# Flamingo block on one core: the softmax sums of the two query halves on separate PSUM rows, with every engine's order rewritten

## The reference, cut to what matters

```python
x = x + tanh(g_xattn[0]) * attention(layernorm(x), ctx, Wq, Wkv_expand, Wout)   # 16 batches x 256 x 512
x = x + tanh(g_ffn[0])   * ffn(layernorm(x), w_gate, w_up, w_down, ...)         # fp8-rounded, width 1408
# attention: 16 heads of 32, 256 queries, 256 keys, causal
scores = einsum('bhqd,bhkd->bhqk', qh, kh) / sqrt(32)
scores = where(tril, scores, lowest)
attn = softmax(scores, axis=-1)        # exp, then divided by its sum over the keys
out = einsum('bhqk,bhkd->bhqd', attn, vh)
```

## Time and profile before

| | |
|---|---|
| median of three runs | 728.0 us |
| the profiled execution | 729.19 us |
| its span, first to last instruction | 727.4 us |
| mean granted TensorE clock | 0.978 of full speed |
| busy share: PE, DVE, ACT, POOL | 90%, 93%, 76%, 74% |

### The profile page before, as it was taken

The page is one execution under the profiler, slowest core; times in us unless marked ns, Lnnn a source line. Parts: engine busy times, 40 slices in busy tenths (PEclk is TensorE's granted clock), DMA queues, the critical chain, the costliest instruction groups (busy, mean ns, idle before and its releaser), DMA issues.

```text
span 727.4 us, 15637 instructions
## 1 busy us (share of the span) xinstructions
PE 657.9 (90%) x6091; PEld 419.9 (58%) x6160; DVE 680.1 (93%) x1127; ACT 555.5 (76%) x995; POOL 538.5 (74%) x601
## 2 busy tenths in 40 slices
PE   1758698999999999999999999999999999998794
PEld 1647476666566666566565657566566556545342
DVE  4999998989899999999999999999999999999997
ACT  6896878987869787878878787979797867555642
POOL 6768889796968778687878686968696677666651
PEclk9888999999999999999999999999999999999997
DMA  8887768385795757585867566675775686512121
GB/s 303 223 153 199 157 147 176 80 176 94 123 158 107 152 105 154 80 181 96 167 108 141 111 144 116 132 144 114 155 123 116 90 150 100 111 22 87 27 70 58
DMA packets 143479, 93.57 MB, mean 129 GB/s; under 512 B 107598, under 2 KB 114126, under 8 KB 143406
## 3 DMA queue, kind: packets, MB, share of 16 engines
q1 hardware_dynamic: 141246, 90.74, 61.6%
q0 software_dynamic: 576, 1.45, 0.8%
q10 hardware_dynamic: 1584, 0.39, 0.3%
HBM read 31.59 MB, written 9.83 MB: 57 GB/s over the span
## 4 chain that ended last, share of the span: by engine, by line
PE 47%; DVE 29%; POOL 11%; DMA 5%; issue 3%; ACT 3%; SPq 0%; ACTq 0%; DVEq 0%
PE pair L1153 26%; DVE mx L3116 5%; POOL PT L793 4%; PE pair L1411 4%; PE pair L1416 3%; DVE room L2943 2%; DVE room L2947 2%; PE pair L1394 2%; DVE room L3260 2%; PE pair L1440 2%; DVE room L3308 2%; PE pair L1436 2%; POOL room L832 2%; DVE tm L3323 2%; DVE wmax L2962 2%
## 5 line engine op out<-in xcount | busy, mean ns | idle before, releaser
L832 POOL TENSOR_TENSOR room<-room,up_scale 128x512 f32<-128x512 f32 (+1 forms) x96 | 125.6, 1312 | 63.1 <-ACT room L2349 62.2
L3116 DVE TENSOR_REDUCE mx<-pair 128x6 f32<-128x768 f32 x128 | 117.6, 947 | 1.7 <-PE pair L1343 1.4
L793 POOL TENSOR_SCALAR_AFFINE_SELECT PT<-PT 128x512 f32<-128x512 f32 x128 | 104.0, 841 | 13.1 <-ACT PT L2274 13.0
L2274 ACT ACTIVATE PT<-pair 128x768 f32<-128x768 f32 x128 | 98.3, 814 | 9.4 <-PE pair L1394 7.8
L1153 PE MATMUL pair<-WgT,room 128*128 128x512 bf16 (+1 forms) x382 | 89.5, 366 | 2.5 <-DVE room L3447 0.8
L1153 PE MATMUL pair<-xT,WqTh 128*128 128x256 bf16 x512 | 86.5, 272 | 1.5 <-ACT WdT L2037 1.3
L1153 PE MATMUL pair<-WuT,room 128*128 128x512 bf16 (+1 forms) x368 | 84.8, 361 | 3.3 <-DVE room L3260 1.4
L2349 ACT ACTIVATE room<-room,sx 128x512 f32<-128x512 f32 (+1 forms) x96 | 65.2, 682 | 24.2 <-DVE room L3260 18.8
L1153 PE MATMUL pair<-WdT,room 128*128 128x512 bf16 x326 | 75.4, 379 | 3.1 <-DMA room<-room 2.9
L2381 ACT ACTIVATE room<-room 128x512 bf16<-128x512 f32 (+1 forms) x96 | 55.8, 586 | 21.2 <-DVE room L3308 21.1
L1153 PE MATMUL pair<-xT,WqTl 128*128 128x256 bf16 x256 | 69.7, 272 | 0.0
(11 more groups left out here) (151 smaller groups left out, 1863.4 us busy)
## 6 DMA issues: line engine op xcount, KB each, us to landing
xin<-in_x_dram SPq DMA_DIRECT2D x16, 512.0 KB, 4.0
x<-in_x_dram SPq DMA_DIRECT2D x16, 512.0 KB, 4.8
K<-kh SPq DMA_DIRECT2D x32, 256.0 KB, 4.9
Q<-qh SPq DMA_DIRECT2D x32, 256.0 KB, 4.6
out_dram<-x SPq DMA_DIRECT2D x15, 512.0 KB, 3.0
K<-kl SPq DMA_DIRECT2D x16, 256.0 KB, 6.1
Q<-kl SPq DMA_DIRECT2D x16, 256.0 KB, 4.2
room<-in_L_ffn_w_down_dram SPq DMA_DIRECT2D x4, 704.0 KB, 9.0
```

What stands on the lines that cost most here:

```text
L793: pool.affine_select(out=view, in_=view, compare_op=ALU.is_ge, fill=0.0, base=0, pattern=[[0, 2], [0, 2], [1, P]], channel_multiplier=-1). ...
L832: pool.tensor_tensor(g, g, up_scale[:, chunk(n)[1]], ALU.mult).then_inc(slw_done, 1)
L2274: act.activation(head_columns(ring(b, c), 0, 384), head_columns(shifted_pair[c][:, :], 0, 384), ACT.Exp, scale=SCALE).then_inc(exp_done, 1)
L3116: dve.tensor_reduce(mx[:, heads, :], head_columns(w, 0, 3 * P).rearrange("p h (r s) -> p h r s", s=P), AX.X, ALU.max).then_inc(max_done, 1)
```

## The change

The sums of queries 0 to 127 and of queries 128 to 255 no longer lie side by side in 256 columns, but on different rows of the same 128 columns. `pick` has eight variants instead of four, with a 1 in every eighth column. Variant g serves queries 0 to 127, variant 4+g serves queries 128 to 255. The diagonal pattern comes from a flat tile that is read with rows of 33. The number of streamed columns per head group is the same (1536 over the four column tiles), now in twelve matmuls of 128 columns instead of four of 256 and four of 128. The reciprocal has 128 columns instead of 256, and eight shuffles of 128 columns take the place of four of 256.

```diff
-        pick = sb("pick", [P, KT, HD])
+        pick_flat = sb("pick_flat", [P, TT * KT * (HD + 1)])
...
-        rsum = sb("rsum", [P, S])
+        rsum = sb("rsum", [P, P])
...
+        pick = pick_flat[:, 0:TT * KT * HD].rearrange("p (v c) -> p v c", c=HD)
+        pick_ones = pick_flat[:, :].rearrange("p (v c) -> p v c", c=HD + 1)
...
-            constant(pool.memset(pick[:, :, :], 0.0))
-            for g in range(KT):
-                constant(pool.memset(pick[:, g, :].rearrange("p (a b) -> p a b", b=4)[:, :, g:g + 1], 1.0))
+            constant(pool.memset(pick_flat[:, :], 0.0))
+            for a in range(HD // (TT * KT)):
+                constant(pool.memset(pick_ones[:, :, TT * KT * a:TT * KT * a + 1], 1.0))
...
-                for t in range(TT):
-                    for j in range(G):
-                        last = pe.matmul(sum_bank[HD * j:HD * j + HD, t * P:S], pick[:, g, :],
-                                         probabilities(b, 2 * g + j // 2, j % 2, t), start=(g == 0 and t == 0),
-                                         stop=(g == KT - 1 and t == TT - 1), skip_group_check=True)
+                for j in range(G):
+                    pe.matmul(sum_bank[HD * j:HD * j + HD, 0:P], pick[:, g, :], probabilities(b, 2 * g + j // 2, j % 2, 0)[:, 0:P],
+                              start=(g == 0), stop=False, skip_group_check=True)
+                for j in range(G):
+                    pe.matmul(sum_bank[HD * j:HD * j + HD, 0:P], pick[:, KT + g, :], probabilities(b, 2 * g + j // 2, j % 2, 0)[:, P:S],
+                              start=False, stop=False, skip_group_check=True)
+                for j in range(G):
+                    last = pe.matmul(sum_bank[HD * j:HD * j + HD, 0:P], pick[:, KT + g, :], probabilities(b, 2 * g + j // 2, j % 2, 1),
+                                     start=False, stop=(g == KT - 1), skip_group_check=True)
...
-                dve.reciprocal(rsum[:, :], sum_bank[:, 0:S]).then_inc(rsum_done, 1)
+                dve.reciprocal(rsum[:, :], sum_bank[:, 0:P]).then_inc(rsum_done, 1)
...
-                dve.stream_shuffle(out=R[:, 2 * h, :], in_=rsum[:, :], mask=[2 * h] * HD)
-                dve.stream_shuffle(out=R[:, 2 * h + 1, :], in_=rsum[:, :], mask=[2 * h + 1] * HD).then_inc(r_spread, 1)
+                for g in range(2 * h, 2 * h + 2):
+                    for t in range(TT):
+                        last = dve.stream_shuffle(out=R[:, g, tok(t)], in_=rsum[:, :], mask=[KT * t + g] * HD)
+                last.then_inc(r_spread, 1)
```

```diff
             x_low(3, 1)
             unit_rounded(13)
-            down_placed(7)
             down_placed(1)
-            unit_rounded(15)
-            down_placed(6)
+            down_placed(3)
+            rstd2_made(0)
             normalised_low(1, 0)
...
```

Some PSUM banks of the weight preparation and of the last batch's turning are others (`turned_bank`, `turned_x_bank`, `aw_bank`, `s_bank`, `w_bank`), and a few waits come or go with the order. One of them is on PE:

```diff
-                if n == 4 and b <= 10:
+                if n == 4 and 2 <= b <= 11:
                     pe.wait_ge(t_done, 6 * b + 1)
```

More of the change, by code:

```diff
@@ L834, in added @@
             def added(b, t):
+                if t == 0 and b == 0:
+                    pool.wait_ge(y_done, 1)
+                if t == 0 and b == 9:
+                    pool.wait_ge(y_done, 19)
                 if t == 0 and b >= 12:
@@ L986, in _ @@
             added(0, 1)
+            up_scaled(1, 5)
             causal_part(3, 2)
@@ L1105, in _ @@
             causal_part(14, 7)
+            rstd2_made(13)
             up_scaled(12, 5)
+            normalised_low(14, 0)
             added(12, 0)
-            normalised_low(14, 0)
             normalised_low(14, 1)
-            rstd2_made(13)
             up_scaled(13, 0)
@@ L1711, in _ @@
             values(3, 1)
+            gate_products(1, 0)
             down(0, 0)
+            scores(3, 0)
+            scores(3, 1)
             up_products(1, 0)
-            scores(3, 0)
-            gate_products(1, 0)
-            scores(3, 1)
+            projected(2, 0)
             scores(3, 2)
-            projected(2, 0)
             projected(2, 1)
@@ L1721, in _ @@
             scores(3, 3)
+            scores(3, 4)
             keys(4, 1)
-            scores(3, 4)
             gate_products(1, 1)
@@ L1861, in _ @@
             scores(13, 3)
+            keys(14, 0)
+            scores(13, 4)
+            keys(14, 1)
             projected(12, 1)
-            scores(13, 4)
-            keys(14, 0)
-            keys(14, 1)
             scores(13, 5)
+            scores(13, 6)
+            queries(14, 0)
+            scores(13, 7)
             gate_products(11, 1)
-            scores(13, 6)
             gate_products(11, 2)
-            scores(13, 7)
-            queries(14, 0)
+            up_products(11, 1)
+            gate_products(11, 3)
             queries(14, 1)
-            up_products(11, 1)
+            gate_products(11, 4)
+            turned_maxima(13)
+            up_products(11, 2)
             queries(14, 2)
-            up_products(11, 2)
-            turned_maxima(13)
-            gate_products(11, 3)
-            gate_products(11, 4)
             queries(14, 3)
@@ L1948, in _ @@
             down(12, 0)
-            up_products(13, 0)
             scores(15, 1)
+            gate_products(13, 0)
             scores(15, 2)
-            gate_products(13, 0)
+            scores(15, 3)
             projected(14, 0)
-            scores(15, 3)
             scores(15, 4)
@@ L1958, in _ @@
             scores(15, 6)
+            up_products(13, 0)
+            scores(15, 7)
             gate_products(13, 1)
-            scores(15, 7)
             up_products(13, 1)
+            gate_products(13, 2)
             values(15, 1)
-            gate_products(13, 2)
+            turned_maxima(15)
             gate_products(13, 3)
-            turned_maxima(15)
+            up_products(13, 2)
+            projected(14, 2)
             gate_products(13, 4)
-            projected(14, 2)
-            up_products(13, 2)
             gate_products(13, 5)
@@ L2478, in _ @@
-            unit_taken(5)
-            unit_abs(8)
-            unit_abs(10)
+            unit_abs(7)
+            unit_taken(5)
+            means1(2, 0)
+            keys_high(1, 0)
+            c_high(2)
+            keys_high(1, 1)
+            unit_abs(9)
+            squares1(2, 0)
+            means1(2, 1)
+            keys_exact(1, 0)
+            unit_taken(6)
+            keys_exact(1, 1)
+            squares1(2, 1)
+            unit_abs(10)
+            unit_abs(8)
+            unit_taken(7)
@@ L2584, in _ @@
             exps(2, 1)
+            abs_t(0, 2)
+            queries_high(3, 1)
             exps(2, 2)
```

2468 lines of the change are left out of this document (1257 added, 1211 removed).

## The result

The changed kernel takes **739.4 us** (median of 4 runs, 737.83 to 740.92), beside 728.05 us of the kernel before on the same chip (4 runs, 727.83 to 728.42). The ratio is 1.0155, with a 95% interval from 1.0133 to 1.0177: slower by 11.3 us. The prediction said 725.7 us, 722.5 to 730.3, and gave slower the smallest chance.

What follows compares the result with a forecast made beforehand. It took PE to bound the middle (140 to 580 us) and DVE the stretch from 580 to 720 us. Terms -1.4 - 0.5 + 0.3 - 0.7 = -2.3 us took the median from 728.0 to 725.7 us, range 722.5 to 730.3.

Steps and rivals of the forecast that it cites:

- The sums: DVE's reciprocal and shuffles: 0.48 us saved a batch, worth 1.4 us in batches 13 to 15 and 0.5 at the head.
- the forecast of +0.3 for PE: PE-bound stretch: 128-column rounds cost 0 to 0.01 us more per group, over about 44 groups.
- The order in the loop: Waits in the loop: at most 2.4 us to gain from PE's idle time, taken as 0.
- The rival on the other side: A new loop wait, where `gate_products(b, 4)` needs a bank DVE reads: 728.5 to 731 us, chance 0.20.
- DVE has 1.7 us to spare in a period: Middle of the kernel: PE sets the pace with 0.3 us idle, so DVE time saved there is worth nothing.
- The head: Before the loop: POOL's shorter list gives -0.7 us (bounds 0 and -4.3), the sums of batches 0 and 1 -0.5.
- The scatters go later, where POOL idles 4 us in 20: POOL ahead of the loop: the scatters moved later fall in idle time; no cost was put on them.
- The end: DVE-bound last stretch: batches 13, 14 and 15 save 0.48 us each, 1.4 us in all.
- What would have shown it wrong: Loop period off 38.4 us by over 0.1, or the stretch before the loop moved by over 2 us.
- The rival of the slower shuffles: 128-column shuffles still take 345 ns: last three batches lose 1.7 us, the first 0.6; about 729 us, chance 0.05.
- no step is added or dropped: Premise of the order's term, all engines: it is only about waits; -0.7 us, bounds 0 and -4.3.

Runs made afterwards that it cites:

- plain_sums: plain_base with only the new sums (matmuls, reciprocal, shuffles), every engine's order as before: 723.76 us, 3.6 us under plain_base.
- delay_ahead: plain_base with one unused 0.6 us reduction added on DVE per loop round, straight ahead of the residual: 730.45 us, period 38.85 us.
- delay_behind: plain_base with the same unused reduction on DVE per loop round, straight behind the residual: 732.53 us, period 38.85 us.
- light_pool: changed_again with POOL's first gate product of each loop round cut to 8 of its 512 columns: 735.5 us, period 38.49 us.
- plain_base: The kernel before with its transposing DMAs replaced by plain DMAs of the same bytes: 727.39 us, ratio 0.9991 to before.
- plain_ahead: changed_again with the residual moved ahead of the rounding subtraction in DVE's loop: 734.88 us, period 38.57 us.
- both_moves: plain_ahead with two scatters of down weights on POOL before the loop moved behind the low keys and two gate products: 740.21 us.
- order_alone: plain_base with the changed orders and banks of all engines but the sums of before: 738.72 us, 11.3 us over plain_base.
- changed_again: The changed kernel with plain DMAs in place of the transposing ones, in its second run on another chip: 740.76 us, ratio 1.0175 to before.

## Why the prediction was wrong, step by step

**The sums: right.** The reciprocal (0.96 for 0.953), the shuffles (1.64 for 1.70 us) and PE's share (0.65 for 0.66 us a group) came out as worked out. DVE saves 3.18 - 2.64 = 0.54 us a batch; 0.48 was forecast. The places were right as well, head and end. The term was mis-sized: -1.6 us for it, and plain_sums measured -3.6. By its parts both places gave more than forecast, 2.3 us for 0.5 up to batch 3 and 3.3 for 1.4 at the end. But these parts are of single executions, and at the end 1.3 us of scatter is seen without any edit, so which of them holds the difference stays open. In the loop the forecast of +0.3 for PE came out as +0.2.

**The order in the loop: the step that failed.** The prediction took 0 there and gave as reason that PE's idle 0.3 us is the hand-over between kinds of matmul. It looked for what can be gained from idle time, and not for what a new order can lose. The runs showed in its place a stall of PE on the residual of 0.54 us and a smaller one on the maxima: a period longer by 0.76 us, 8 x 0.76 = 6 us. The rival on the other side had the right mechanism and even the right price ("each 0.1 us of it costs 0.8 us over eight rounds", which delay_ahead confirms with 0.38 us a round and 3.1 us in all), but the wrong place and size. It checked `gate_products(b, 4)`, with 1.7 us of slack, and `turned_maxima`, given about 1 us. It didn't check `gate_products(·, 1)` against the residual, where the trace of before shows some 0.2 us. And delay_behind shows that the slack of the maxima was 0.2 us too. A wait with such a margin leaves no row in the view of waits, which is why that view doesn't name it.

**"DVE has 1.7 us to spare in a period": true and of no use.** The sum of idle time is right. But both delays of 0.6 us cost 0.38, so only some 0.2 of the spare 1.7 us lies between the scores and what PE takes back from DVE. For the same reason the 0.54 us that the new sums free didn't help: in after DVE waits 0.38 of them out for scores, and 39.23 is as long as 39.21 without them.

**What made the path longer.** Of the 0.82 us that it grew (4.87 to 5.69), the subtraction is 0.75. light_pool, which touches POOL alone, takes this back, and with it the whole stall: 38.49 us, the period of plain_base. plain_ahead takes the residual out of the path instead and reaches 38.57. So the cause of the loss in the loop is shown, from both ends. The prediction costed DVE's instructions as if each had one duration. The earlier trace rows bear that out for shuffles and for operations on PSUM, but not for one with two SBUF inputs.

**The head: -0.7 forecast (and -0.5 from the sums), +5.3 measured.** "The scatters go later, where POOL idles 4 us in 20" failed as a statement on the trace, for two of them stand in front of products that DVE waits for. But both_moves shows that this wait isn't what costs the time. order_alone has the same head (reciprocal of batch 3 at 204.0 us; 199.2 in plain_base, 204.5 in after), so it is the order, and neither the sums nor the transposes. Which step of it, stays open. The chain of waits offers a reading, which is argued and not tested: in before DVE holds it nearly alone from 41 to 68 us, and in after it runs there through ScalarE's copies, POOL's `rstd` (2.82 us at 38.18) and TensorE, which waits 4.5 us for `x` (L1237).

**The end.** -0.7 us for the -1.4 forecast, in one profiled execution of each. From batch 11 on plain_base and delay_ahead, with the same orders there and the old sums, have 218.7 and 217.4 us, so a difference of 1.3 can be chance. plain_sums has 215.5. The new order has 216.9 with the old sums (order_alone) and 214.9 to 217.0 with the new ones. So it isn't shown that the new order costs anything here, nor how much of the sums' gain is left in it.

**What would have shown it wrong** was named: a period off by more than 0.1 us (it is 0.76), a stretch ahead of the loop off by more than 2 us (it is 5.3), "then the order, not the sums, made the time". order_alone against plain_base, +11.3 us, confirms it. The rival of the slower shuffles was added up wrongly beside this: 728.0 + 1.7 + 0.6 + 0.3 - 0.7 is 729.9, and not 729. It changes nothing, as the shuffles are as cheap as forecast. The range was too narrow because the order's term had no bound upwards: "no step is added or dropped" was read as "no cost".

**A better version.** plain_sums is faster than plain_base by 3.6 us, so the new sums in the old order should beat both kernels, by some 0.5%. With the transposing DMAs it was not run, so that it does is inferred from this pair.

## What to carry to other kernels

When a change rewrites the order of several engines, take each place where the bound engine takes back a buffer, note when it wants it and when the other engine is through, and treat a margin of a few tenths as a wait: a list of waits shows only those already lost. Test an edit and the new order apart, and don't add the two results up: the new sums were worth 3.6 us in the old order and nothing in the new one, which lost 11.3 by itself. And where two engines hold each other up, as DVE's subtraction and POOL's product did here, a piece of work of the one with time to spare belongs beside operations that it doesn't hold up (the maxima took 0.67 us either way); where it can't be moved, let the instruction that somebody waits for go first.

## What the runs showed of the hardware

The subtraction of 128x512 from f16 to bf16 takes 0.41 us alone, 0.88 us beside a stream of POOL's products, and 1.38 us in the loop of after. This is not a slower rate: in the loop the subtraction ends 0.28 us after POOL's product, however long it has then been running, and in a dense run of such subtractions it is POOL that waits (3.72 us for a product of 1.26). Over the 32 subtractions of the kernel the mean went from 666 to 736 ns with the transposes in place. With plain DMAs it is 769 ns in changed_again, and 542 in light_pool, where POOL's one product per round was cut. In DVE's busy time this waiting counts as work: changed_again has 681.6 us of it, and light_pool 670.7. So a part of the 92% was waiting.
